# Gated delta rule with experts: the last two heads reordered, the last head's outputs normed and added in two halves

## What is computed

```python
x = x + attn_ref(xn, ...) + ffn_ref(xn, ...)
# attn_ref, for each head:
qkvz = hidden @ W_qkvz;  mixed = silu(causal_conv4(q, k, v))
M = -tril((k_beta @ k.T) * decay, -1)            # chunks of 64 in the reference
T = solve_triangular(eye - M, eye, lower=True)
v_new = T @ v_beta;  k_cumdecay = T @ (k_beta * exp(g))
def step(state, inp):
    vn  = v_i - k_cumdecay_i @ state
    out = (q_i * exp(g_i)) @ state + attn @ vn
    state = state * exp(g_last) + (k_i * exp(g_last - g_i)).T @ vn
    return state, out
x = core * silu(z)
x = x * rsqrt(mean(x * x, -1) + EPS) * norm_weight
return x @ W_out
```

## Time and profile before

| | us |
|---|---|
| median of 3 runs (1569.88 to 1573.05) | 1571.14 |
| the profiled execution | 1573.48 |
| its span, first to last instruction | 1571.7 |
| PE busy in it | 1525.4 |
| round 13, last with all three kinds, `solved(13, 0)` to `solved(14, 0)` | 58.95 |
| round 14, `solved(14, 0)` to `solved(15, 0)` | 59.00 |
| round 15 from `solved(15, 0)` to the last add | 35.8 |

### The profile page before, as it was taken

One profiled execution on the slowest core, in us unless ns is written; L12 is line 12 of the kernel. 1 busy time (PEld: TensorE's weight loads), 2 busy tenths in 40 slices (PEclk: granted clock), 3 DMA queues, 4 the chain that ended last, 5 costly groups with the idle time before them and its releaser, 6 DMA issues.

```text
span 1571.7 us, 29150 instructions
## 1 busy us (share of the span) xinstructions
PE 1525.4 (97%) x10922; PEld 1078.0 (69%) x10922; DVE 1107.6 (70%) x2449; ACT 777.1 (49%) x1672; POOL 442.5 (28%) x279
## 2 busy tenths in 40 slices
PE   6999999999999999899999999999999999999987
PEld 4766676766656775666866866866866866866856
DVE  5454454565375435598898898898898898898874
ACT  3444444345423334565665665565565565565531
POOL 1000000005043004254354354354253253253211
PEclk9999999999999999999999999999999999999998
DMA  4343442213324333323423323323323323323210
GB/s 133 97 147 97 153 164 76 69 58 119 109 86 125 121 100 106 97 58 82 104 59 81 105 55 85 103 59 83 87 60 71 87 56 75 87 59 66 58 18 27
DMA packets 225051, 136.88 MB, mean 87 GB/s; under 512 B 160976, under 2 KB 196304, under 8 KB 224912
## 3 DMA queue, kind: packets, MB, share of 16 engines
q1 hardware_dynamic: 221840, 126.62, 29.6%
q0 software_dynamic: 3072, 8.39, 1.7%
HBM read 94.85 MB, written 35.91 MB: 83 GB/s over the span
## 4 chain that ended last, share of the span: by engine, by line
PE 92%; DVE 4%; issue 2%; ACT 1%; DMA 1%; POOLq 0%; POOL 0%; SPq 0%; DVEq 0%; ACTq 0%
PE ps L923 8%; PE ps L818 7%; PE ps L579 7%; PE ps L839 7%; PE ps L674 4%; PE ps L604 4%; PE ps L1059 4%; PE ps L708 4%; PE ps L860 3%; PE ps L746 3%; PE ps L594 3%; PE ps L893 3%; PE ps L756 3%; PE ps L1082 3%; PE ps L870 3%; PE ps L892 2%
## 5 line engine op out<-in xcount | busy, mean ns | idle before, releaser
L1389 ACT ACTIVATE vs<-ps 128x256 f32<-128x256 f32 x128 | 49.1, 383 | 259.0 <-PE ps L860 254.6
L2292 POOL TENSOR_TENSOR qg<-qT,Ebc 128x1024 f32<-128x1024 f32 x32 | 74.8, 2358 | 353.3 <-PE ps L893 353.3
L1884 DVE SCALAR_TENSOR_TENSOR cv<-ps,cw,cv 128x1022 f32<-128x1022 f32 (+2 forms) x96 | 122.7, 1279 | 17.6 <-ACT cv L1336 13.7
L923 PE MATMUL ps<-wout,xT 128*128 128x256 f32 x512 | 128.9, 396 | 2.2 <-DVE total L1994 2.2
L1994 DVE SCALAR_TENSOR_TENSOR total<-ps,rr,total 128x256 f32<-128x256 f32 x256 | 118.9, 481 | 9.9 <-POOL rr L2298 3.0
L1895 DVE SCALAR_TENSOR_TENSOR cv<-ps,cw,cv 128x1022 f32<-128x1022 f32 (+2 forms) x96 | 122.6, 1277 | 2.3
L839 PE MATMUL ps<-xnT,gz 128*128 128x512 f32 x256 | 122.3, 602 | 0.7 <-DVE cv L1884 0.6
L818 PE MATMUL ps<-xnT,gv 128*128 128x512 f32 x256 | 118.8, 607 | 0.5
L579 PE MATMUL ps<-xrT,cv 128*128 128x512 f32 x256 | 117.8, 593 | 1.1 <-ACT xrT L1233 0.8
L1296 ACT ACTIVATE we<-ps,bias 128x128 f32<-128x128 f32 (+3 forms) x128 | 65.7, 525 | 98.2 <-DVE bias L1704 98.2
L923 PEld LDWEIGHTS ps<-wout,xT 128*128 128x128 f32 x512 | 93.2, 192 | 28.3 <-issue 12.6
(11 more groups left out here) (256 smaller groups left out, 3569.4 us busy)
## 6 DMA issues: line engine op xcount, KB each, us to landing
xs_dram<-zeros SPq DMA_DIRECT2D x16, 1024.0 KB, 7.6
dec<-grow_dram SPq DMA_DIRECT2D x32, 512.0 KB, 4.8
Ebc<-erow_dram SPq DMA_DIRECT2D x32, 512.0 KB, 5.0
cv<-in_wqk SPq DMA_DIRECT2D x16, 512.0 KB, 3.6
xn<-xs_dram SPq DMA_DIRECT2D x47, 128.0 KB, 2.1
ys_dram<-yg SPq DMA_DIRECT2D x47, 128.0 KB, 1.9
we<-in_we SPq DMA_DIRECT2D x16, 352.0 KB
cv<-in_wv SPq DMA_DIRECT2D x16, 256.0 KB, 3.6
```

The source lines that it names most:

```text
L923: last = mm(ps[:, output_bank(t), r * H:(r + 1) * H], xT[:, r, t * P:(t + 1) * P], wout[:, r, :], start=True, stop=True)
L1884: ins = stt(row, pair(bank)[:, :, 0:S - k], cw[:, f, i, TAPS - 1 - k:TAPS - k], row, ALU.mult, ALU.add)
L2292: tt(qg[:, r], qT[:], Ebc[:, r], ALU.mult).then_inc(fl["g_qg"], 1)
```

## The change

Only rounds 14 and 15 are changed, by new branches in the loops (`elif middle` for round 14, `else` for round 15).

- DVE, round 14: the residuals of step 3 come after solve row 9 instead of row 11. The convolution of r = 0 comes before `output_lengths`, all three transposes `turned_diagonal` before the convolution of r = 1, `second_values` goes (ACT does it: `last_values`), and the copy of the last block (`blocks_of_128`) before the adds of tiles 5 to 7.
- POOL, round 14: `decayed_queries` also waits for v_base, the end of the solve.
- PE, round 14: both `project_values`, then `output_squares`, and only then `first_blocks`; the output products are spread otherwise, tile 7 after the last block products.
- ACT: `take_value` r = 0 ahead of the squares, both `values` ahead of the copies of `beside_32`; `last_values` ahead of the last copy into PT.
- Output products of rounds 14 and 15 use other banks (`output_bank(h, t)`, `last_bank`).
- Round 15: squares, lengths, norms and adds in two halves. Half 0 is the chunks m = 0, 1 of both batches (tiles 0, 1, 4, 5), half 1 the rest; `LAST` is the order of the tiles in products, adds and stores. `last_squares(0)` stands ahead of `solved(15, 3)`.

A second definition of `load_rows` and `store_rows` that shadowed an equal one is also gone; no instruction of SP changes by it.

```diff
+        LAST = (0, 1, 4, 5, 2, 3, 6, 7)
+        def last_bank(i, r):
+            return (5, Y, Y + 1, 5, 2, 3, Y, r * (Y + 1))[i]
...
+            def last_squares(m):
+                pe.wait_ge(fl["a_x"], 4 * (NK - 1) + 2 * m + 2)
+                if m:
+                    pe.wait_ge(fl["v_sxt"], NK)
+                for j in range(4):
+                    cols = slice(j * BL, (j + 1) * BL)
+                    for r in range(R):
+                        src = sqb[:, r, :, cols].rearrange("p (b t) n -> p b t n", b=B)[:, :, 2 * m:2 * m + 2, :]
+                        last = mm(ps[cols, X, (2 * m + r) * P:(2 * m + r + 1) * P], ones[:], src, start=True, stop=True)
+                last.then_inc(fl["p_sx"], 1)
+            def last_products(a, z):
+                for i in range(a, z):
+                    if 0 < i < 3:
+                        pe.wait_ge(fl["v_add"], 8 * (NK - 1) - 2 + i)
+                    if i == 3:
+                        pe.wait_ge(fl["v_add"], 8 * (NK - 1) + 1)
+                    if i == 4:
+                        pe.wait_ge(fl["v_g"], 4 * NK)
+                    if i >= 6:
+                        pe.wait_ge(fl["v_add"], 8 * (NK - 1) + i - 4)
...
+                    if h == NK - 2:
+                        if t == 2:
+                            pe.wait_ge(fl["a_vs"], NK)
+                        if t >= 4:
+                            pe.wait_ge(fl["v_add"], 8 * h + t - 3)
...
+            def last_values():
+                act.wait_ge(fl["p_vt"], 2 * NK)
+                for t in range(NT):
+                    last = fn(vs[:, 1, t, :], tiles(X)[:, t, :], ACT.Copy, scale=nk2[:, (NK - 1) % 2, t:t + 1])
+                last.then_inc(fl["a_vs"], 1)
...
+            def last_lengths(m):
+                cols = slice(2 * m * P, 2 * (m + 1) * P)
+                dve.wait_ge(fl["p_sx"], NK + m)
+                dve.transpose(sxt[:].rearrange("p u c -> p (u c)")[:, cols], ps[:, X, cols]).then_inc(fl["v_sxt"], 1)
...
+                for r in range(R):
+                    src = sxt[:, 8 * m + 4 * r:8 * m + 4 * r + 4, 0].rearrange("p (b t) -> p b t", b=B)
+                    last = stt(of_half(sxv[:], m)[:, r], src, 1.0 / D, half_epsq, ALU.mult, ALU.add)
+                last.then_inc(fl["v_sx"], 1)
...
                 if middle:
-                    solve_rows(8, 12)
+                    solve_rows(8, 12 if ahead else 10)
...
+                else:
+                    add_last(0, 2)
+                    last_lengths(1)
+                    add_last(2, NT)
...
+            def last_norms(m):
+                pool.wait_ge(fl["v_sx"], NK + m)
+                pool.wait_ge(fl["v_add"], 8 * (NK - 1))
+                tt(of_half(rr2[:], m), of_half(sxv[:], m), half[:, 1, 0:NT].rearrange("p (r b t) -> p r b t", r=R, b=B),
+                   ALU.pow).then_inc(fl["g_rr"], 1)
...
+                    if not ahead:
+                        pool.wait_ge(fl["v_base"], NK)
                     decayed_queries(n)
```

More of the change, by code:

```diff
@@ L1559, in _ @@
                     silu_key(f)
+                if middle and not ahead:
+                    take_value(n, 0)
                 if scan:
@@ L1588, in _ @@
                     beside_64(n)
+                if middle and not ahead:
+                    last_values()
                 if ahead:
@@ L2144, in _ @@
                     system(n, 0)
-                if scan:
+                if scan and middle:
                     blocks_of_128(h)
@@ L2148, in _ @@
                     system(n, 1)
-                if scan and h:
+                if scan and middle and h:
                     add_outputs(h - 1, 7, NT)
```

169 lines of the change are left out of this document (106 added, 63 removed).

## The result

| | before | changed |
|---|---|---|
| median, us | 1570.53 (1569.88 to 1573.05, 4 runs) | 1560.84 (1559.47 to 1562.27, 4 runs) |
| profiled execution, us | 1573.48 | 1560.70 |
| its span, us | 1571.7 | 1558.9 |

The ratio is 0.9934, with a 95% interval of 0.9919 to 0.9950: 9.7 us less by the medians, 12.8 us by the profiled executions. Timed a second time beside the kernel before (9 runs, median 1573.45), the changed kernel had 1559.82 in 5 runs, a ratio of 0.9912 (0.9898 to 0.9925), 13.6 us. The forecast was 13.3 us less and 1557.8.

A forecast was written before the change was run, and what follows sets the result against it. PE was busy 97%, so only its idle and slow time in rounds 14 and 15 could go. Round 14 7.3 + step 0 2.6 + tail 5.4 = 15.3, less 2 for a clock fall, 13.3 us: 1571.14 to 1557.8; range 1553.8 to 1562.

The forecast's parts named there:

- step 0: First step of round 15: 4.3 us instead of 6.92 without the fall of the clock, 2.6 us saved.
- The copy and POOL: End of round 14's solve: with POOL waiting, DVE's copy takes 0.37 us instead of 2.54, its DMAs come 1.65 earlier.
- rival 3: Solve's copy is slow for its own reason, what follows comes 2.2 us later: 11.1 us gained, 1560.0; chance 0.05.
- The old wait of 5.21: PE idle ahead of first_blocks in round 14: filled with work that stood behind it, no clock fall there.
- The new wait: PE in round 14 ahead of beside_32, for DVE's transposes after the PT DMAs: 2.1 us, start at 1512.9.
- The wait for tile 4: PE in round 14: products of tile 4 wait 1.4 us for DVE's add of tile 0.
- rival 1: Clock never falls in the changed rounds: 15.3 us gained, 1555.8; chance 0.24.
- Rival 2: Clock low for 6.8 us or twice, also in step 0: 8.7 or 9.5 us gained, 1561.6 to 1562.4; chance 0.14.
- Rival 6: Change does nothing, as one chain (values, convolution, adds) sets the end of round 14 as before: 1571; chance 0.02.
- rival 5: Short waits keep PE at the lower clock from 1513 through round 15: 12 us slower, 1583; chance 0.03.
- Tail: From solved(15, 3) to the last add: 12.6 us instead of 18.23, 5.6 less 0.25 for squares, 5.4 saved.
- Rival 4: Halves do not come apart in the tail, its gain shrinks to about 1: 8.9 us gained, 1562.2; chance 0.07.

The follow-up runs named there:

- solve_rows_back: Changed kernel with round 14's solve rows and step 3 residuals in the old order; on another chip, 1567.82 us, ratio 0.9916 to the kernel before.
- no_base_wait: Changed kernel without POOL's wait for v_base ahead of its decayed queries of round 14; 1564.36 us, ratio 0.9941 to the kernel before.
- values_behind: Changed kernel with first blocks and squares again between the two value projections on PE in round 14; 1563.94 us, ratio 0.9936 to the kernel before.
- second profile: Profile of the changed kernel run once more, unaltered; k3 to last add 60.28 us, median 1559.82, ratio 0.9912 to the kernel before.
- round14_alone: Changed kernel with the old tail, so only round 14 is new; 1564.34 us, ratio 0.9944 to the kernel before.
- tail_alone: Kernel before with the new tail in halves and the old round 14; 1566.47 us, ratio 0.9955 to the kernel before.
- base_wait_alone: Kernel before with only POOL's wait for v_base added in round 14; 1569.64 us against 1573.22 beside it, ratio 0.9971.

## Why the prediction was right, step by step

The mechanism held in its main steps. That the clock fell exactly once, and that step 0 counted in full, was luck, as said below.

Times of the changed kernel are given less 1.24 where they stand beside forecast ones.

- **Bound.** PE idle and slow time in rounds 14 and 15 gave the time. From k3 on, 75.45 us had 14.5 of idle time before; the changed kernel has 61.40 - 55.83 = 5.6. The prediction names three stretches with a clock below 1.00, but the earlier trace rows has five; its sum used all five.
- **Residuals.** The wait of 0.98 became 0.34 (0.27 forecast). The last `chunk_output` ended at 1498.54 (1498.5) and the copy started at 1500.13 (1500.05). All as forecast, but this step brought PE 0.7 us at the price of 0.5 us for the copy, and `solve_rows_back` shows no gain from it.
- **The copy and POOL.** 0.37 us, rival 3 falls. The ports were at work in more than the copy, as `no_base_wait` showed; the step stands since the new wait shields both.
- **The old wait of 5.21.** Gone, with its fall of the clock; `values_behind` brings both back, for 4.1 us.
- **The new wait.** Forecast at 2.1, measured 2.52. `beside_32` started at 1513.65 against 1512.9: the four issues took 1.92 us instead of 2.99, but the last transfer landed 3.6 after its issue, not 1.9. The 1.9 was the lowest landing of the earlier trace rows, whose median is 2.5. In the second profile the issues took 3.03, and PE's idle time was 1.64 ahead of P22BD, where the forecast has 0.2, and 0.66 here. So neither execution has the waits as forecast: the first has a longer one here (2.52, just over the 2.5 that was to be the limit), the second the forecast's 2.3 us in all, but most of it ahead of P22BD.
- **The wait for tile 4**, forecast at 1.4: 0.86 where the clock was full, none where it had fallen and PE came late, which is how part of the fall is taken back.
- **The clock.** One fall of some 3.4 us in the first profile, as forecast, and none in the second. k3 to s0 was 5.7 us shorter with it and 6.85 without; forecast were 5.3 and 7.3. So rival 1 and the forecast are both executions of this kernel, and my 2 us for a fall are 1.1 in the difference of these two. That the first profile had exactly the one fall that was forecast is luck. Rival 2 did not come in the changed kernel, but in `round14_alone` the clock was low for some 10 us behind a wait of 2.08.
- **Step 0.** 4.31 us (4.3). Right in size, wrong in standing: `tail_alone` has the same gain with the waits in place, and `base_wait_alone` part of it (16.66 from s0 to s3, against 17.59). It counts in full only against an execution of before like the profiled one.
- **`last_values`.** Eight on ACT took 2.18 us, not 4.0; PE did not wait for them. Rival 6 falls with k3 to s0, rival 5 with PEclk 1.00 through round 15.
- **Tail.** 12.25 against 12.6, saved 5.98 against 5.6, and the squares of half 0 cost 0.26 (0.25). The prediction put nothing of it to the clock, and no run separates the two. Rival 4 falls: DVE has no gap over 0.25 us from the first add on.

The sum in its own execution is 5.72 + 2.35 + 5.98 = 14.05, against the forecast of 13.3. Against the profiled execution the forecast was 1560.2, and 1560.70 came: the sum was 0.75 us too small, and the 1.24 us ahead of k3 took that back and more. What failed is the last step to the median, 2.3 us taken off because three runs of before had 1571.14 where its profiled execution had 1573.48. The changed kernel's median lies 0.14 us above its profiled execution, so it came out at 1560.84 and not at 1557.8. By the first comparison the gain is 7.9 to 12.7 us, which leaves 13.3 out; beside nine runs of before it is 11.8 to 16.0.

Before itself varies with its clock: of those nine runs the shortest, 1569.66, had a mean granted clock of 0.991, and the six with 0.987 took 1573.43 to 1575.35. A gain that is partly spared falls of the clock depends on how many of them the runs of before happen to have, and three or four runs do not settle it.

The chances of the rivals leave at most 0.12 outside the range, not 0.12 to 0.15, and the upper end of rival 2, 1562.4, lies outside it too.

## What to carry to other kernels

When the last rounds of a software pipeline run out of work, give them an order of their own: put the independent products ahead of the ones that wait for a round trip through DRAM, and split a final chain of sum, norm and add so that its first half runs under the last step. Look at the row beside a slow instruction of DVE before giving it a reason: if POOL started just ahead of it, a wait for which POOL has time can shorten the critical chain, here by 3.6 us with two lines. Count separately what a shorter wait gives and what a clock that doesn't fall gives; the second comes and goes between executions of the same program.

## What the runs showed of the hardware that I had not expected

- POOL's multiplications held up a DVE multiplication of 128 x 225 as well (2.18 us against 0.40) and after it the copy (1.98 against 0.37), one behind each half, while the reduction between them kept its 0.39.
- The same two waits (0.78 and 1.49 us) brought the clock down in two profiles and not in a third, and a wait of about 2 us ahead of `beside_32` was followed by some 3.4 us at the lower level in two kernels (2.52 and 1.95) and by some 10 us in another (2.08).
- Of the four PT transfers, which SP issues in a row, one is late by about a microsecond or more in each of the twelve profiles: in nine an issue took 1.3 to 1.8 us instead of 0.45 (2.79 to 3.30 us for the four), and in the other three (1.92 for the four) one transfer landed 3.0 to 3.6 us from its issue instead of 1.9.
- `key_state(14, 3)`, with the same instructions ahead of it in every kernel, started between 1493.2 and 1495.6 us on one chip and between 1501.5 and 1504.7 on another, a spread as large as what most of the edits here are worth.
